# Two more adjacency loads ahead of a store, and the whole seventh block ahead of a gather, in a two-step graph attention kernel

## The reference

```python
R = S + jnp.eye(N); R = R / R.sum(-1, keepdims=True)
Xf = Xa = X
for n in range(2):
    q = Xa @ W1.T @ W2.T; k = Xa @ W3.T
    probs = softmax(q @ k.T)              # 4096 x 4096
    A = probs kept per row, largest first, while the sum before it is < 0.9; rows rescaled to 1
    Xf = R @ Xf
    Xa = A @ Xa
    Z = Z + Xf @ U1[n].T + Xa @ U2[n].T
h = X + Z, layer norm of h; result = layer norm of (x + that)
```

## Time and profile before

| | |
|---|---|
| median of 3 runs | 1667.79 us (1663.79 to 1667.81) |
| profiled execution, its time | 1664.64 us |
| profiled execution, its span | 1662.8 us |
| PE busy | 1531.0 us, 92% of the span |
| DVE busy | 1266.9 us, 76% |
| ACT busy | 779.7 us, 47% |
| POOL busy | 244.0 us, 15% |
| granted TensorE clock, mean | 0.956 |

### The profile page before, as it was taken

The page is one execution under the profiler, slowest core; times in us unless marked ns, Lnnn a source line. Parts: engine busy times, 40 slices in busy tenths (PEclk is TensorE's granted clock), DMA queues, the critical chain, the costliest instruction groups (busy, mean ns, idle before and its releaser), DMA issues. The chain is left out here.

```text
span 1662.8 us, 17981 instructions
## 1 busy us (share of the span) xinstructions
PE 1531.0 (92%) x4753; PEld 887.4 (53%) x4753; DVE 1266.9 (76%) x3735; ACT 779.7 (47%) x1237; POOL 244.0 (15%) x283
## 2 busy tenths in 40 slices
PE   7999999979999999998999999998259879899996
PEld 4556556434555555554566666565135445455553
DVE  6788888723677777776799999999868787787664
ACT  4555555412556565564444444444134434445444
POOL 2010210241000000001001111112310221312222
PEclk9999999989999999998999999999569999999998
DMA  7556566644444555555556766672000000000000
GB/s 266 176 154 155 154 171 188 192 180 140 166 173 187 208 208 188 185 202 205 187 155 200 190 182 186 178 177 79 3 2 1 1 8 7 1 7 7 7 7 13
DMA packets 53452, 211.94 MB, mean 127 GB/s; under 512 B 22464, under 2 KB 31232, under 8 KB 32880
## 3 DMA queue, kind: packets, MB, share of 16 engines
q1 hardware_dynamic: 49872, 210.61, 40.7%
q0 software_dynamic: 3488, 0.31, 0.2%
HBM read 206.64 MB, written 4.50 MB: 127 GB/s over the span
## 5 line engine op out<-in xcount | busy, mean ns | idle before, releaser
L1289 ACT ACTIVATE psL<-psL,umax 128x1024 f32<-128x1024 f32 x256 | 278.5, 1088 | 297.1 <-DVE umax L1812 297.0
L1818 DVE MAX8 cand<-psL 128x8 f32<-128x256 f32 (+1 forms) x640 | 372.4, 584 | 57.4 <-PE psL L916 52.1
L915 PE MATMUL psL<-kA,mq 128*128 128x512 f32 x512 | 299.5, 585 | 2.5 <-ACT psL L1289 1.6
L885 PE MATMUL psO<-adj_in,xn 128*128 128x512 f32 x512 | 242.7, 597 | 3.8 <-DMA adj_in<-in_adjT 2.1
L885 PE MATMUL psO<-adj_in,xf 128*128 128x512 f32 x512 | 241.9, 597 | 4.4 <-POOL adj_in L611 4.4
L1097 PE MATMUL psO<-ebuf,xn 128*128 128x512 f32 x512 | 241.5, 593 | 0.5 <-DVE ebuf L2029 0.5
L2029 DVE SCALAR_TENSOR_TENSOR ebuf<-ebuf 128x1024 f32<-128x1024 f32 x128 | 156.7, 1225 | 109.0 <-PE psO L1097 92.2
L1449 ACT ACTIVATE ebuf<-psL 128x1024 f32<-128x1024 f32 x128 | 130.5, 1022 | 187.8 <-PE psL L1143 153.4
L916 PE MATMUL psL<-kB,mq 66*128 66x512 f32 x512 | 203.8, 398 | 0.0
L1398 ACT ACTIVATE ebuf<-psL 128x1024 f32<-128x1024 f32 x128 | 130.9, 1023 | 129.3 <-PE psL L1064 128.9
L1155 PE MATMUL psO<-xf,xa 128*128 128x512 f32 x340 | 167.6, 617 | 5.7 <-DVE xf L2182 5.6
(11 more groups left out here) (341 smaller groups left out, 1962.3 us busy)
## 6 DMA issues: line engine op xcount, KB each, us to landing
adj_in<-in_adjT SPq DMA_DIRECT2D x128, 1024.0 KB, 5.0
adj_in<-in_adj SPq DMA_DIRECT2D x32, 2048.0 KB, 7.6
xaT<-in_xT SPq DMA_DIRECT2D x4, 512.0 KB, 5.4
xa_dram<-xa SPq DMA_DIRECT2D x8, 256.0 KB, 7.8
out<-t SPq DMA_DIRECT2D x8, 256.0 KB, 2.3
list_dram<-ids,place POOLq DMA_INDIRECT x64, 9.3
rel_prob<-cut_dram SPq DMA_DIRECT2D x32, 2.0 KB
cut_dram<-ncut SPq DMA_DIRECT2D x16, 2.0 KB, 8.8
```

The lines of the kernel that those rows point to most:

```text
L885: last = nc.tensor.matmul(psO[:], fs[:, j, :], adj_in[:, r % RING, j % JQ, :], start=(j == 0), stop=(j == JT - 1))
L915: nc.tensor.matmul(o, qA[:, t * P:(t + 1) * P], kA[:, c:c + BI], start=True, stop=False)
L1289: nc.scalar.activation(ps[:], ps[:], ACT.Exp, bias=umax[:, bass.ds(i * UB + k, 1)], scale=1.0, accum_out=usum[:, bass.ds(i * UB + k, 1)]). ...
L1818: last = v.max(cand[:, t % 2, at + c * 8:at + c * 8 + 8], psL[(turn + k) % 3][:, c * WIDE:(c + 1) * WIDE])
```

## The change

`EARLY_LOADS` goes from 2 to 4. Hence `held` goes from 54 to 56: SP issues the loads of parts 54 and 55 ahead of `rank_store(7)` and of the wait for `h_x`. A condition keeps the store of the last block from being issued a second time by the loop at n = 54. In PE's program the same constant sets how many parts of the seventh block stand ahead of the wait for `counted` and of `prepare_q(0)`: six before, all eight now, through these two loops:

```diff
-        EARLY_LOADS = 2
+        EARLY_LOADS = 4
...
                     for n in range(held):
                         flow_load(n)
-                        if n >= 12 and n % FLOWS == 0:
+                        if n >= 12 and n % FLOWS == 0 and (n - 12) // FLOWS < NB - 1:
                             rank_store((n - 12) // FLOWS)
                     rank_store(NB - 1)
```

## The result

The changed kernel took 1679.59 us (median of 6 runs, 1675.18 to 1682.28) against 1667.80 us for the kernel before (6 runs): a ratio of 1.0077, 95% interval 1.0059 to 1.0094, which is 10 to 16 us longer. The forecast was 1681.

What follows compares the result with a forecast made beforehand. The stage was taken as bound by the sequence gathers, preparation, DVE, with PE's parts as long as their cover. Terms 0.9 + 4.3 + 9.8 - 1.5 = 13.5 us longer gave 1678.1, said as 1681 in the median; range 1675 to 1686.

Steps and rivals of the forecast that it cites:

- The wait for the identity: PE cannot begin part 54 until POOL's `add_self(6)` is done, 4.3 us after the gathers' arrival (3.9 to 4.6).
- The two parts: Parts 54 and 55 on PE, now ahead of the preparation, partly at the low clock: 9.8 us (9.2 to 10.4).
- The preparation: First preparation up to `guess`, reached by PE at full clock: 8.6 us, a gain of 1.5 (2.1 gained to 0.6 lost).
- The stores: SP's last stores go out later behind the two loads, so POOL's href waits 0.9 us (0 to 1.8).
- a late list: POOL's list scatters run beside SP's loads and might land late: 2.3 us, kept only for the range.
- What it gives back: Less PE work behind the preparation gives 1.9 to 5 us of idle time ahead of DVE's flag, worth nothing.
- Sum: All terms together: 13.5 us longer, 11.0 to 17.4, and 19.7 with the list late.
- The rival that the parts fit into the hole: Both parts run in PE's 7.98 us hole before the gathers; not slower, 1666.6 us in the median; chance 0.04.
- The heavier rival: List or stores come much later, or PE stays at low clock through all parts: 18 to 22 us longer; chance 0.09.
- absorbed: Rival that half of the delay is absorbed at `guess` or the stage's end: 5 to 11 us longer; chance 0.06.

Runs made afterwards that it cites:

- experiment 2: Kernel before with only PE's order changed (parts 54 and 55 ahead of the first preparation), SP's program as before: ratio 1.0072, 9 to 15 us longer.
- experiment 4: Changed kernel with `add_self` of the seventh block ahead of the reading of the list on POOL: ratio 1.0022 to the kernel before, 1 to 6 us longer.
- the two traces: Both kernels were run and traced again: the kernel before took 1662.84 us in one run, the changed kernel had ratio 1.0099 to it.
- experiments 1: Kernel before with only the loads of parts 54 and 55 ahead of the last store, PE's order as before: ratio 1.0027, 2 to 7 us longer.
- experiment 3: Changed kernel with the last block's three stores ahead of the loads of parts 54 and 55: ratio 1.0094 to the kernel before, 12 to 19 us longer.
- experiments 5: Kernel before with its last block's three stores ahead of the load of part 53: ratio 0.9992, no difference that can be told.
- experiments 6: Changed kernel with the last block's three stores ahead of the loads of parts 53, 54 and 55: ratio 1.0100 to the kernel before, 14 to 20 us longer.
- experiments 7: Changed kernel with stores ahead of the loads of parts 53 to 55 and the seventh block's `add_self` ahead of the list's reading: ratio 1.0015 to before.
- experiments 10: Changed kernel with the last block's cut store (512 pieces of 4 bytes) issued twice: ratio 1.0105, beside 1.0099 for the changed kernel.

## Why the prediction was right

The forecast of 13.5 us stands against 12.8 (ratio 1.0077) and 16.5 (ratio 1.0099) measured, and against 15.8 between the means of the last row of the table. The mechanism was the one forecast for all but the stores, whose term was 3.2 us too small; two other terms, 1.2 us too long together, hid part of that. That 13.5 lies between the two measured values is therefore in part luck. Step by step:

- **The wait for the identity**: forecast 4.3 us behind the gathers, measured 4.4 (364.79 - 360.40) and 4.7. Experiments 2 and 4 show it from both sides: PE's order alone costs 9 to 15 us, and with the identity early no more is left than the loads alone cost.
- **The two parts**: forecast 9.8 us, measured 9.2 and 9.6 from PE's release to the first transpose. At full clock they take 7.03, so 2.3 us were lost to the low clock, at the lower end of what I had allowed. The granted clock was 0.50 from 364.8 to 369.0 and 1.00 from 370.0. The Trainium skill, TensorE: Matmul & The Clock Gate, section "What's actually happening", calls the slow clock the state that activity lifts; the trace agrees, with 9.37 us for the 16 rows behind the idle time of 17.75 us, but filling the hole was worth little: in experiment 4, where it is filled, PE still fell idle for 5.56 us and its preparation took 11.1 us.
- **The preparation**: forecast 8.6 us, measured 8.0 twice, against 10.1 and 10.5 before. That is what the rows at the full clock alone had given (1.84 + 6.2), of which I had taken a little more. It gained 2.3 us between the means, where I had said 1.5 and at most 2.1.
- **The stores**: this step was mis-sized and put in the wrong place. I said that href would wait 0.9 us for them. What waited was the read of the list, which landed together with them: 10.25 us for 1 KB. PE was therefore idle for 17.75 us, where I had said 12 to 13. The gathers came 4.1 us later between the means of the table's first row, outside the 0 to 1.8 given for the term, and as much as both upper ends together (1.8 and 2.3 for a late list), though the list itself was early. The error was to look only at the explicit wait for the stores (`cut_out`), and not at the small read issued while they were under way.
- **What it gives back**: nothing, as forecast. PE had 3.65 us of idle time ahead of the flag (forecast 1.9 to 5), and the half block had one stretch at the low clock in it (15.60 us for 13.90).
- **Sum**, by the means of the two traces: 4.1 + 4.5 + 9.4 - 2.3 = 15.7 us, and `guess` began 49.1 - 33.5 = 15.6 us later. Against 13.5 the stores gave 3.2 us more and the identity 0.2, the parts 0.4 and the preparation 0.8 less. The ratio of the first comparison, 12.8 us, lies below this and that of the second, 16.5, above.

The rival that the parts fit into the hole is refuted in the change. Experiment 4 shows its condition: with the identity early the parts do fit, though even then the kernel was 1 to 6 us longer and not as short as the rival had it, because of the late read. The heavier rival was right in its first half only, by some 4 us. Nothing was absorbed: `guess` is 15.6 us later and L1054 15.8.

## What to carry to other kernels

Before work is moved into a hole of an engine, follow its inputs one by one: one small operation on another engine, queued behind the very event that ends the hole, turned 7 us of hidden work into 9 to 15 us on the critical chain. Look behind the moved work too, at what had been ready and now stands in the queue. And of transfers moved ahead of small stores, ask not only who waits for these stores, but which small transfers will be in flight at the same time.

## What was not expected of the hardware

- A read of 1 KB landed after 2.0 us in the kernel before, where it was issued at 346.75 and the last store had landed at 344.6, and after 9.9 us when it was issued 3 us behind three stores of 2 KB each, and that with the DMA engines at a share of 0.00 for most of the time. The stores themselves landed after 11.8 to 12.7 us. The Trainium skill, DMA: Bandwidth & Descriptors, section "Queues, rings and completion order", says that the increment of a semaphore lands only after every earlier write of its DMA engine, across the queues; the landing of the read within 0.3 us of the last store, here and in experiments 1 and 4, agrees with it.
- Doubling the 512 pieces of 4 bytes changed nothing in that (9.9 us again for the read). Of the stores' 12 us the first 4 have a reason in the trace: the load of part 55, issued just ahead of them, was being moved until about 344.7, and of the 844 packets between 343 and 345 us 775 were under 512 bytes; the three stores have 768 pieces. From 347 to 355 us no packet moved at all, and why the stores, issued from 340.57 on, landed only from 352.4 to 354.3 was not found.
- Putting the stores ahead moved the lateness to others: in experiment 3 the scatters of the list landed after 10.1 to 11.1 us, and the load of part 54, issued behind the stores, after 12.1 us, where that of the changed kernel, 4 us ahead of them, had taken 6.0. A load issued just ahead of them is not safe either: that of part 55 in the changed kernel took 12.6 us, and in experiments 5 to 7 PE waited for one issued 3.5 us ahead.
- How late the list was read, counted from the end of the last scatter, goes with both stores and loads: 4.3 to 5.0 us where the scatters go ahead of the stores (the changed kernel in both traces, experiments 1 and 10), 7.5 to 9.1 where the stores go ahead but not the two loads (the kernel before in both traces, experiments 2 and 5), 11.1 and 12.6 where both do (experiments 3 and 6). No run separates the two further.
